# A graph layer on one core: second chunk in halves, early casts on GpSimd, issues spread, and unread products on TensorE

## The reference

```python
bw = sign(weight)
ba = maximum(sign(x), 0)          # 1 where x > 0, else 0
xw = ba @ bw.T                    # N x D, whole numbers
out = relu(adj @ xw)
y = x + out
result = (y - mean(y)) / sqrt(var(y) + 1e-5)      # over each row of 256
```

## Time and profile before

| | |
|---|---|
| runs | 991.89, 992.87, 993.97 us; median 992.87 |
| profiled execution | 991.81 us, span of its instructions 989.9 us |
| TensorE | 972.1 us busy (98%) |
| VectorE, GpSimd, ScalarE | 847.3 (86%), 839.8 (85%), 613.5 us (62%) |
| moved | 294.69 MB, mean 298 GB/s |
| chain that ended last | PE 97%, DVE 1%, DMA 1% |

### The profile page before, as it was taken

One profiled execution on the slowest core, in us unless ns is written; L12 is line 12 of the kernel. 1 busy time (PEld: TensorE's weight loads), 2 busy tenths in 40 slices (PEclk: granted clock), 3 DMA queues, 4 the chain that ended last, 5 costly groups with the idle time before them and its releaser, 6 DMA issues.

```text
span 989.9 us, 12378 instructions
## 1 busy us (share of the span) xinstructions
PE 972.1 (98%) x4548; PEld 806.7 (81%) x4548; DVE 847.3 (86%) x879; ACT 613.5 (62%) x655; POOL 839.8 (85%) x360
## 2 busy tenths in 40 slices
PE   5999999999999999999999999999999999999997
PEld 4888888888888888888888888888888888888886
DVE  5868998989888898988989898898988989898894
ACT  3877675665656566565665656566565656656562
POOL 2567998988889889898998889899888998889893
PEclk9999999999999999999999999999999999999999
DMA  9999999999999999999999999999999999999971
GB/s 306 348 341 318 322 318 323 278 312 299 321 294 291 296 312 317 288 312 306 288 297 303 324 282 308 304 315 314 288 319 287 313 295 305 319 281 308 307 204 43
DMA packets 296428, 294.69 MB, mean 298 GB/s; under 512 B 9392, under 2 KB 296368, under 8 KB 296368
## 3 DMA queue, kind: packets, MB, share of 16 engines
q1 hardware_dynamic: 156640, 155.34, 57.2%
q10 hardware_dynamic: 139728, 138.56, 49.7%
HBM read 285.47 MB, written 8.39 MB: 297 GB/s over the span
## 4 chain that ended last, share of the span: by engine, by line
PE 97%; DVE 1%; DMA 1%; issue 0%; ACT 0%; ACTq 0%; DVEq 0%
PE ps L554 93%; PE ps L628 1%; PE ps L530 1%; DMA raw<-in_adj_dram 1%; PE ps L520 1%; PE ps L592 1%; PE ps L548 0%; ACTq L182 0%; DVE ps L392 0%; ACT hi L279 0%; DVE stats L404 0%; DVE rows L481 0%; PE ps L616 0%; DVE xw L445 0%; DVE lo L396 0%
## 5 line engine op out<-in xcount | busy, mean ns | idle before, releaser
L259 POOL TENSOR_TENSOR lo<-turned,hi 128x1024 fp32r<-128x1024 f32 x351 | 838.7, 2412 | 135.1 <-ACT hi L279 131.1
L554 PE MATMUL ps<-hi,xw 128*128 128x512 f32 x2016 | 787.1, 390 | 0.0
L554 PE MATMUL ps<-lo,xw 128*128 128x512 f32 x2016 | 784.7, 389 | 0.0
L279 ACT ACTIVATE hi<-turned 128x1024 fp32r<-128x1024 f32 x351 | 372.3, 1062 | 255.8 <-PE ps L554 173.6
L554 PEld LDWEIGHTS ps<-hi,xw 128*128 128x128 f32 x2016 | 378.5, 188 | 78.0
L554 PEld LDWEIGHTS ps<-lo,xw 128*128 128x128 f32 x2016 | 378.5, 188 | 77.9
L392 DVE STREAM_TRANSPOSE turned<-raw 128x1024 f32<-128x1024 f32 x351 | 425.1, 1218 | 0.0
L396 DVE TENSOR_TENSOR lo<-ps,hi 128x1024 fp32r<-128x1024 f32 x161 | 196.5, 1220 | 106.3 <-ACT hi L279 106.3
L279 ACT ACTIVATE hi<-ps 128x1024 fp32r<-128x1024 f32 x161 | 165.1, 1026 | 89.9 <-PE ps L554 77.2
L392 DVE STREAM_TRANSPOSE ps<-raw 128x1024 f32<-128x1024 f32 x161 | 196.2, 1219 | 3.8 <-DMA raw<-in_adj_dram 3.8
L296 ACT ACTIVATE rows<-rows,shift,rstd 128x256 f32<-128x256 f32 x62 | 36.3, 586 | 0.6 <-DVE shift L415 0.6
(11 more groups left out here) (38 smaller groups left out, 109.8 us busy)
## 6 DMA issues: line engine op xcount, KB each, us to landing
raw<-in_adj_dram SPq DMA_DIRECT2D x254, 512.0 KB, 11.1
raw<-in_adj_dram ACTq DMA_DIRECT2D x254, 512.0 KB, 12.0
rows<-in_x_dram SPq DMA_DIRECT2D x16, 512.0 KB, 10.7
out_dram<-rows SPq DMA_DIRECT2D x15, 512.0 KB, 15.8
x_sb<-in_x_dram SPq DMA_DIRECT2D x14, 256.0 KB, 10.2
x_sb<-in_x_dram ACTq DMA_DIRECT2D x14, 256.0 KB, 11.9
raw<-in_adj_dram SPq DMA_DIRECT2D x4, 256.0 KB, 7.0
raw<-in_adj_dram ACTq DMA_DIRECT2D x4, 256.0 KB, 7.8
```

The lines of the kernel that those rows point to most:

```text
L259: pool.tensor_tensor(lo[:, n % RING], turned[:, ordinal(n) % TP], hi[:, n % RING].bitcast(f32), ALU.subtract).then_inc(p_los_made, 1)
L279: act.activation(hi[:, n % RING], src, ACT.Copy).then_inc(his_made, 1)
L554: return pe.matmul(acc[b % 2][a], xw[:, step, a * P:(a + 1) * P], part[:, n % RING, k * MB:(k + 1) * MB], start=(step == 0 and part is hi) ...
```

## The change

- Chunk 1 is loaded in halves like chunk 0 (`HALVED = 2`), so units 4 to 7 are used as 16 half products each. Its `x` comes as two pieces, one per group. The order of loads is x 0, half 0, x 1, half 1, x 2, half 2, x 3, half 3. Half 3 is issued when one unit has been turned.
- For chunks 2 to 7 the issue steps move: x(c,h) to unit 4(c - 2) + 2h, adj(c,h) one unit later than before. They alternate, one issue of each queue per unit. On ScalarE they stand behind the step's copy and cast.
- The casts of groups 1 and 2 are on GpSimd. The copy of `xw` group 0 moves from VectorE to ScalarE; copies of groups 0 to 3 stand one step of ScalarE earlier.
- GpSimd makes `ident_b` before `ident`. TensorE makes 30 products of `ident_b` with itself at the start, and 8, 10, 24 and 4 more between its first real steps. They are written into a bank that unit(0) then starts anew; nobody reads them.

```diff
+    HALVED = 2
+    X_PIECES = [(g * GK, GK) for g in range(HALVED * UPC // UPG)] + [(c * KB, KB) for c in range(HALVED, CH)]
...
-            early = 4 + 2 * half if ch < CH else max(CH + 3 - ch, 0) + half
+            early = 5 + 2 * half if ch < CH else max(CH + 3 - ch, 0) + half
             return max(UPC * (ch - SLOTS + 1) + early, 0)
         def x_at(c, half):
-            return max(UPC * c - 9 + 2 * half, 0)
+            return UPC * (c - HALVED) + 2 * half
...
         def _(sp):
-            for i in range(2):
+            for i in range(2 * HALVED):
                 start_x(sp, i, LOWER)
-                start_half(sp, i, LOWER)
+                if i < 2 * HALVED - 1:
+                    start_half(sp, i, LOWER)
+            sp.wait_ge(units_turned, 1)
+            start_half(sp, 2 * HALVED - 1, LOWER)
...
         def _(pool):
+            for g in range(1, EARLY_CASTS):
+                pool.wait_ge(x_loaded[g], G * 16)
+                if g >= STEP_BUFS:
+                    pool.wait_ge(casts_turned, g - STEP_BUFS + 1)
+                pool.tensor_copy(cast_x[:, g % STEP_BUFS], x_sb[:, g * GK:(g + 1) * GK]).then_inc(pool_casts, 1)
...
         def _(act):
             for n in range(UNITS):
                 make_hi(n)
+                if n < UB:
+                    g = n // UPG
+                    if n % UPG == (0 if g < HALVED * UPC // UPG else 1):
+                        copy_xw(g)
+                    if n % UPG and EARLY_CASTS <= g + 2 < GROUPS:
+                        cast(g + 2)
+                if n == 0:
+                    start_half(act, 2 * HALVED - 1, UPPER)
...
-                if n < UB:
-                    g = n // UPG
-                    if n % UPG and g >= 1:
-                        copy_xw(g)
-                    if n % UPG and g + 2 < GROUPS:
-                        cast(g + 2)
...
         def _(dve):
             turn(0)
-            dve.wait_ge(xw_made, 1)
-            dve.tensor_copy(xw[:, 0:GK], ps_xw).then_inc(xw_copied, 1)
-            first_cast(1)
             make_lo(0)
...
         def _(pe):
+            def keep_warm(count):
+                for _ in range(count):
+                    pe.matmul(acc[0][0][:, 0:P], ident_b[:], ident_b[:], start=True, stop=True)
+            pe.wait_ge(idents_made, 1)
+            keep_warm(30)
...
-                if n < UPC:
+                if n < HALVED * UPC:
...
+            keep_warm(8)
             turn_step(0)
+            keep_warm(10)
             pe.wait_ge(signs_copied, 1)
             make_xw(0)
+            keep_warm(24)
             turn_step(1)
+            keep_warm(4)
```

More of the change, by code:

```diff
@@ L39, in build @@
     STEP_BUFS = 2
+    EARLY_CASTS = 3
     BACK_AT = 4
@@ L58, in ordinal, with piece_of_chunk @@
         return before[kinds[n]][n]
-    X_PIECES = [(0, GK), (GK, GK)] + [(c * KB, KB) for c in range(1, CH)]
+    HALVED = 2
+    X_PIECES = [(g * GK, GK) for g in range(HALVED * UPC // UPG)] + [(c * KB, KB) for c in range(HALVED, CH)]
     def piece_of_group(g):
-        return g if g < KB // GK else g * GK // KB + 1
+        return [i for i, (first, count) in enumerate(X_PIECES) if first <= g * GK < first + count][0]
+    def piece_of_chunk(c):
+        return X_PIECES.index((c * KB, KB))
     adj_v = adj.rearrange("(b t i) (c g k) -> b c g i t k", t=NT, i=Q, c=CH, g=G)
@@ L120, in build @@
         x_loaded = [sem(f"x_loaded{i}") for i in range(len(X_PIECES))]
-        halves_loaded = [sem(f"halves_loaded{i}") for i in range(2)]
+        halves_loaded = [sem(f"halves_loaded{i}") for i in range(2 * HALVED)]
         adj_loaded = [sem(f"adj_loaded{s}") for s in range(SLOTS)]
@@ L131, in build @@
         signs_copied = sem("signs_copied")
-        first_casts = sem("first_casts")
+        first_cast = sem("first_cast")
+        pool_casts = sem("pool_casts")
         casts_made = sem("casts_made")
@@ L171, in start_half @@
         def start_half(eng, i, quadrants):
-            t0, t1 = i * NT // 2, (i + 1) * NT // 2
+            ch, t0 = i // 2, i % 2 * NT // 2
             for g in quadrants:
-                eng.dma_start(raw_view(0)[g * Q:(g + 1) * Q, t0:t1],
-                              adj_v[0, 0, g, :, t0:t1]).then_inc(halves_loaded[i], 16)
+                eng.dma_start(raw_view(ch)[g * Q:(g + 1) * Q, t0:t0 + NT // 2],
+                              adj_v[0, ch, g, :, t0:t0 + NT // 2]).then_inc(halves_loaded[i], 16)
         def start_x(eng, i, quadrants):
@@ L217, in load_rows @@
                 sp.dma_start(rows[:], x_rows[b]).then_inc(rows_loaded, 16)
-            start_x(sp, 2, LOWER)
-            load_chunk(1)
-            for c in range(2, CH):
+            for c in range(HALVED, CH):
                 for half in range(2):
                     sp.wait_ge(units_turned, x_at(c, half) + 1)
-                    start_x(sp, c + 1, LOWER[half:half + 1])
+                    start_x(sp, piece_of_chunk(c), LOWER[half:half + 1])
                     sp.wait_ge(units_turned, issue_at(c, half) + 1)
@@ L251, in _ @@
             pool.wait_ge(zeroed, 2)
-            for m in (ident, ident_b):
+            for m in (ident_b, ident):
                 pool.affine_select(out=m[:], in_=m[:], compare_op=ALU.not_equal, fill=1.0, base=0,
                                    pattern=[[-1, P]], channel_multiplier=1).then_inc(idents_made, 1)
+            for g in range(1, EARLY_CASTS):
[3 more added lines that the diff above has]
+                pool.tensor_copy(cast_x[:, g % STEP_BUFS], x_sb[:, g * GK:(g + 1) * GK]).then_inc(pool_casts, 1)
             for n in range(UNITS):
@@ L313, in _ @@
             act.activation(warm[:], eps[:], ACT.Copy)
[L314 to L317, removed]
+            for i in range(1, 2 * HALVED):
+                start_x(act, i, UPPER)
+                if i < 2 * HALVED - 1:
+                    start_half(act, i, UPPER)
             for n in range(UNITS):
                 make_hi(n)
-                for c in range(2, CH):
+                if n < UB:
[6 more added lines that the diff above has]
+                    start_half(act, 2 * HALVED - 1, UPPER)
+                for c in range(HALVED, CH):
                     for half in range(2):
                         if n == x_at(c, half):
-                            start_x(act, c + 1, UPPER[half:half + 1])
+                            start_x(act, piece_of_chunk(c), UPPER[half:half + 1])
                 for ch in range(2, NCHUNK):
@@ L328, in _ @@
                             start_chunk(act, ch, UPPER[half:half + 1])
-                if n < UB:
-                    g = n // UPG
-                    if n % UPG and g >= 1:
-                        copy_xw(g)
-                    if n % UPG and g + 2 < GROUPS:
-                        cast(g + 2)
-                else:
+                if n >= UB:
                     ending(n // UB - 1, n % UB)
@@ L368, in turn @@
                 ch, u = n // UPC, n % UPC
-                if ch == 0:
+                if ch < HALVED:
                     if u < 2:
-                        dve.wait_ge(halves_loaded[u], G * 16)
+                        dve.wait_ge(halves_loaded[2 * ch + u], G * 16)
                 elif u == 0:
-                    dve.wait_ge(adj_loaded[ch % SLOTS], (ch // SLOTS + (ch % SLOTS > 0)) * G * 16)
+                    dve.wait_ge(adj_loaded[ch % SLOTS], (ch // SLOTS + (ch % SLOTS >= HALVED)) * G * 16)
                 if kinds[n] == "P":
@@ L436, in ending @@
                     make_shift(b, whole)
-            first_cast(0)
+            dve.wait_ge(x_loaded[0], G * 16)
+            dve.tensor_copy(cast_x[:, 0], x_sb[:, 0:GK]).then_inc(first_cast, 1)
             dve.wait_ge(signs_turned, 1)
@@ L511, in turn_step @@
             def turn_step(n):
-                if n < STEP_BUFS:
-                    pe.wait_ge(first_casts, n + 1)
+                if n == 0:
+                    pe.wait_ge(first_cast, 1)
+                elif n < EARLY_CASTS:
+                    pe.wait_ge(pool_casts, n)
                 else:
-                    pe.wait_ge(casts_made, n - STEP_BUFS + 1)
+                    pe.wait_ge(casts_made, n - EARLY_CASTS + 1)
                 if n >= 2:
```

5 lines of the change are left out of this document (1 added, 4 removed).

## The result

The changed kernel takes 1000.74 us (median of 6 runs, 999.13 to 1002.82) against 993.42 us of the kernel before (6 runs). The ratio is 1.0077, 95% interval 1.0058 to 1.0095. It is slower by 7.3 us (5.8 to 9.4 by the interval), and the forecast (992.8, 990.9 to 994.3) was wrong. The profiled execution took 1001.96 us with a span of 1000.2; the span before was 989.9, so here 10.3 us are to be found.

A forecast was written before the change was run, and what follows sets the result against it. It took fixed TensorE work behind a start to bound the kernel, any gain capped by x(2,1)'s landing. +0.20 - 0.13 = 0.07 us gained gave 992.8 against the median 992.87, range 990.9 to 994.3.

The forecast's parts named there:

- The steps up to unit(5): Start of block 0: unit(0) from 13.6, unit(4) from 26.2, a 1.5 us wait before turn_step(4), unit(5) to 33.0.
- the signs that I had named: Trace marks of a right forecast: x(2,1) ending cast(4)'s wait at 29 to 30 us, make_xw(4) at 36.0 within 0.7.
- Later chunks: Loads behind chunk 2: issues a unit later into queues that stay full, supply gaining 0.5 us a pair; cost nothing.
- C: Rival: GpSimd casts far slower, 5.8 us each giving 994.8; chance 0.03 together with ScalarE's queue running dry.
- DMA order: Loads up to x(2,1): same 8.65 MB in front, landing still 29.49, value 0; bounds 0.7 us either way.
- Casts on GpSimd: Casts 1 and 2 at the start: 2.0 us each, 4.8 as bad case; cast 2 ends by 18.3 even at 2.4.
- Unread products: TensorE's start: a raised clock would return 1.6 us at unit(0), but unit(6) ends the same; priced at 0.
- rival B: Clock falls back at TensorE's waits before unit(1), unit(2), turn_step(4) or unit(6): 2.05 us, giving 994.8; chance 0.05.
- Half products in chunk 1: Units 6 and 7 on TensorE cost 0.08 and 0.05 us more, together 0.13; unit(5)'s are hidden in a wait.
- Rival A: Supply is not the limit, data come earlier: 991.7 (chance 0.10) or, if all supply shifts, 990.0 (chance 0.06).
- small form: Rival A with x(2,1) landing 1 to 1.5 us earlier: some 1.1 us gained, 991.7; chance 0.10.

The follow-up runs named there:

- experiment 1: Changed kernel with ScalarE's DMA issues ahead of the step's copy and cast again, later issue steps kept: 992.76 us, ratio 0.9995.
- experiment 4: Kernel before with only the 76 unread products added and ident_b made first: 993.85 us, ratio 1.0007.
- 5: Changed kernel with the issue steps of the kernel before; ScalarE's issues still behind the step's copy and cast: 992.74 us, ratio 1.0003.
- 7: Changed kernel with ScalarE's issues ahead of copy and cast and without the unread products: 992.5 us, ratio 0.9995.
- experiment 2: Changed kernel without the 76 unread products on TensorE, all else as changed: 1003.26 us, ratio 1.0106.
- Experiment 3: Kernel before with only the issues of chunks 2 to 7 moved: later steps, on ScalarE behind copy and cast: 1002.3 us, ratio 1.0083.
- experiment 10: The kernel of 9 with the change's 76 unread products back: 991.49 us, ratio 0.9986.
- experiment 8: The kernel of 7 with both halves of each chunk's x issued ahead of both halves of its adj: 991.73 us, ratio 0.9986.
- 11: The kernel of experiment 10 with 44 in place of 24 unread products ahead of turn_step(1): 991.49 us, ratio 0.9983.
- 9: The kernel of experiment 8 with the copy of xw group 0 ahead of ScalarE's issues in step 0: 991.24 us, ratio 0.9980.
- experiment 6: Changed kernel, ScalarE's issues first, with all of chunks 2 to 7 issued by SP alone: 1020.63 us, ratio 1.0277.

## Why the prediction was wrong

**Right.** That the kernel ends as many microseconds late as TensorE's last wait of block 0, nothing else; that the landing of x(2,1) bounds what a better start can give; and, for the change without its place of ScalarE's issues, the number: 992.8 forecast, 992.76 measured in experiment 1. That it fits to 0.04 us is luck: x(2,1) landed 1.0 us later there than before, unit(6) started at 35.15 in place of 34.1, and the profiled execution has a span of 991.0 against 989.9; the medians agree because the kernel before was profiled in one of its faster executions. The steps up to unit(5) came in the order said, 0.4 to 1.7 us late: lo(0) ended at 13.83 (forecast 13.45), unit(0) started at 13.98 (13.6), unit(4) at 27.6 (26.2), TensorE waited before turn_step(4) (1.63 us, I had 1.5) and before unit(6) (0.92, I had 1.1). Of the signs that I had named, cast(4) at 29 to 30 us and make_xw(4) at 36.0 failed: they came at 31.17 and 37.77.

```profile
32.28 0.62 PE L540 MATMUL ps<-ident_b,relu 128*128 128x128 bf16 x8 [1.63 <-ACT relu L281]
35.78 0.36 PE L568 MATMUL ps<-hi,xw 128*128 128x256 f32 x1 [0.92 <-POOL lo L273]
```

**The step that failed** is the sentence under "Later chunks": that adj(3,0) stands behind cast(4)'s wait, at 29.5 in place of 24.8, and that "0.79 MB of its queue or 4.5 us at half of 346 GB/s, cover it. Nothing." Three things were wrong in it.
- The cover was counted from the landing of x(2,1). But a landing comes 1.6 us after the bytes have moved by this prediction's own sum; the 0.79 MB behind x(2,1) had been moving since then. Some 2.9 us of the 4.5 were left by that sum. The trace shows less, 0.33 MB, which is 1.9 us at half of 348 GB/s. This is q10 from 31.14 to 36 us:

```profile
q10 hardware_dynamic: 350, 0.33, 23.8%
```

- The wait was put at 29.5. It ended at 31.17. The landing was 1.7 us late, where I had allowed 0.7. About 0.4 of it is a start with 232 GB/s in place of 245 in the first 10 us. For the rest the runs give a hint, no proof: ScalarE issued its part at 18.60, 2.6 us later than before, where I had allowed 1. Where it was issued at 15.8 to 16.7 (before, experiments 1, 4, 5, 7) it landed at 29.5 to 30.5, and where at 18.0 to 18.8 (after, experiments 2, 3) at 30.8 to 31.1. That an issue some microseconds later lands no later, as the prediction says, is thus doubtful.
- A new transfer needs time before its first bytes come. I had 2.2 us for it at the start of the kernel, and left it out here. Here it was some 5 us, from the issues at 31.2 to 32.6 until q10 moved again at 36.5. The next two turns show 5 us again. Why so long is open.

And I did not follow the dependence round. What waits behind cast(4) is not only adj(3,0) but x(3,1), which is what cast(6) waits for. Once the queue runs dry the delay is not paid once but again in each chunk: the forecast gave such a case a chance of 0.03 together with C, and no price of its own; it cost some 8 us (ratio 1.0077 with it, 0.9995 in experiment 1 without). Experiment 3 shows that this alone makes the loss, experiment 1 that without it there is none.

**DMA order, value 0:** the order was right, the bounds were not; the landing went out of them by 1.0 us.

**Casts on GpSimd:** 1.04 us each where I took 2.0; they bound nothing. **Unread products:** 0 gained, as forecast, and rival B's mechanism came, though not at a wait that it named: the clock fell from 2.4 to 1.2 GHz at 14.6 us and was up again at 18.0. The mean of PEclk, 0.83 from 10 to 20 us, shows it; from 14.7 us on the half products of unit(0) were 0.21 us apart:

```profile
10.00:20.00 10.00, 6.82 (x55) 5.68 (x52) 7.03 (x7) 4.51 (x5) 2.48 (x3) 0.83 1.10 347
```

It had been idle 2.40 us before turn_step(1). I had written that it would take a wait longer than 2.21 us. In experiment 4 a wait of 2.08 us, the longest since the unread products began, was followed by the fall (PEclk 0.50 from 13.0 us), and in experiment 10 a wait of 2.29 us at the same step was not. So the length of one wait doesn't decide it. This is turn_step(1) of experiment 4:

```profile
12.65 0.77 PE L526 MATMUL ps<-ident_b,relu 128*128 128x128 bf16 x8 [2.08 <-DVE relu L359]
```

The fall cost nothing because unit(1) waited for lo(1) anyway.

**Half products in chunk 1:** not measured apart. **Rival A** did not come by the change, but experiment 8 shows its condition: bring x(2,1) 3 us forward and the time falls, to 991.73. Its small form said 991.7 for 1 to 1.5 us, so the mechanism is borne out and the equal number is chance.

## What to carry to other kernels

A DMA issue written behind a waiting instruction is a wait of its own: ask which transfer the instruction waits for, and whether what is issued behind it feeds the next such wait; if it does, the loop's length (issue to landing, here 11 to 12 us) is a floor for every turn, and it must be below the compute of a turn. Count the cover from the bytes still to move, not from a landing, and take off the time until the next transfer's first bytes (here some 5 us). And put what the consumer needs first into the queue first, which here was worth 0.8 us (experiment 8 against 7); the unread products were worth nothing that could be told (1 against 7, 10 and 11 against 9).

## What the runs showed of the hardware

- **One queue carries 222 GB/s of these 1 KB packets, two carry 347** (experiment 6), and the DMA share reads 1.10 to 1.13 in both. A full DMA share is no proof of full rate; the GB/s beside it are what counts. That fits the 270 to 285 GB/s of the changed kernel behind 36 us, where the queues take turns at running short; no run tests it apart.
- **A 16 KB transfer of instructions comes earlier where TensorE has the unread products.** In the kernel before 36 of them moved 0.59 MB. In the changed kernel the first (q8) lies in the stretch from 12 to 16 us:

```profile
q8 instruction: 1, 0.02, 1.7%
```

Before, that stretch has none, and the first lies between 28 and 32 us; in the first four experiments it came at 13.2 to 13.8 us with the products (1, 4) and at 25 to 27 without (2, 3). That it delays landings is not shown. In the changed kernel the last quadrant of half 1 on ScalarE's queue took 10.8 us to land where the earlier trace rows have 9.1, but with the transfer nearly as early it took 8.9 in experiment 1 and 9.9 in 10. The landing of x(2,1) is no clearer: with the products it comes 0.3 us later in the changed kernel than in experiment 2, 0.3 later in 1 than in 7, and 1.0 later in 4 than in the kernel before.
